# A transformer decoder on one core: written-out quantised feed-forward stages, and position rounds on two sets of PSUM banks

## What is computed

```python
att_rel_pos = jnp.einsum('bhsd,pd->bhsp', q, pos_emb_k)          # L0 attention
att_pos = jnp.take_along_axis(att_rel_pos, att_idxs[None, None, :, :].astype(jnp.int32), axis=3)
attn_val = jnp.einsum('bhsd,bhtd->bhst', q, k) + att_pos
att = jax.nn.softmax((attn_val + att_pos) * attn_scale, axis=-1)
```

```python
scale = 127.0 / jnp.clip(jnp.max(jnp.abs(x), axis=-1, keepdims=True), 1e-05)
xq = jnp.clip(jnp.round(x * scale), -128.0, 127.0) / scale
...
gate = jax.nn.silu(_bitlinear(x, w_gate))                        # L0 feed-forward
return _bitlinear(gate * _bitlinear(x, w_up), w_down)
...
h = jax.nn.gelu(bitlinear(x, w1, b1), approximate=False)         # L1 feed-forward; bitlinear
return bitlinear(h, w2, b2)                                      # normalises its input by its RMS first
```

## Time and profile before

| | us |
|---|---|
| median of three runs (1726.04 to 1728.31) | 1726.67 |
| the profiled execution | 1730.95 |
| its span, first to last instruction | 1729.2 |
| stage L0a, about | 0 to 252 |
| stage L0f, VectorE's first to last step | 385.5 to 466.9 |
| stage L1f, likewise | 879.5 to 967.3 |

### The profile page before, as it was taken

How to read it: one execution, slowest core, us unless ns; L and a number is a source line. 1 busy time by engine, 2 the same in 40 slices (tenths; PEclk the granted TensorE clock), 3 DMA queues, 4 the chain that set the end, 5 groups by cost and what they waited for, 6 DMA issues and landing times.

```text
span 1729.2 us, 24437 instructions
## 1 busy us (share of the span) xinstructions
PE 1219.0 (70%) x8742; PEld 779.5 (45%) x8754; DVE 1162.2 (67%) x2766; ACT 780.6 (45%) x1466; POOL 225.8 (13%) x170
## 2 busy tenths in 40 slices
PE   4998888974489999799933698987988920000685
PEld 2655555542357777545522354554654410000453
DVE  2655557877667887577767577686775449997354
ACT  1544355764355555346545432665342313442342
POOL 2210101300012233211111000310000000000121
PEclk7888798996789999889967676999999965555698
DMA  3000300000000000000000000000000320001100
GB/s 120 13 13 9 125 27 10 7 1 0 1 1 1 1 1 7 7 7 7 7 1 0 1 1 7 7 8 1 1 0 20 81 57 0 0 0 37 31 13 19
DMA packets 28856, 28.15 MB, mean 16 GB/s; under 512 B 12240, under 2 KB 23504, under 8 KB 27856
## 3 DMA queue, kind: packets, MB, share of 16 engines
q1 hardware_dynamic: 28752, 26.76, 5.3%
HBM read 20.20 MB, written 6.55 MB: 15 GB/s over the span
## 4 chain that ended last, share of the span: by engine, by line
PE 48%; DVE 23%; issue 14%; ACT 9%; POOL 2%; DVEq 2%; DMA 1%; SPq 1%; POOLq 0%; ACTq 0%
PE PSA L898 3%; PE PSA L888 3%; PE PSA L1323 2%; PE PSA L738 2%; DVE BIG L2622 2%; PE PSA L744 2%; PE PSA L721 2%; PE PSA L1005 2%; PE PSA L1017 2%; ACT BIG L1593 2%; PE PSA L1052 2%; DVE BIG L2614 2%; ACT QK L1600 2%; PE PSA L1061 2%; PE PSA L1296 2%
## 5 line engine op out<-in xcount | busy, mean ns | idle before, releaser
L1600 ACT ACTIVATE QK<-PSA 128x512 f32<-128x512 f32 x192 | 104.8, 595 | 110.5 <-PE PSA L898 110.3
L1353 PE MATMUL PSA<-ROWS,ONES 1*128 1x512 f32 x8 | 5.4, 760 | 205.0 <-DVE BIG L2661 205.0
L559 POOL TENSOR_TENSOR RSTD<-VEPS,HALF 128x4 f32<-128x4 f32 x41 | 41.7, 1017 | 649.0 <-DVE VEPS L1951 649.0
L2070 DVE TENSOR_TENSOR BIG<-PSA,MX 128x1024 f32<-128x1024 f32 x96 | 117.6, 1225 | 12.3 <-PE PSA L898 9.4
L888 PE MATMUL PSA<-BIG 32*128 32x512 f32 x384 | 114.6, 687 | 14.8 <-DVE BIG L2070 13.7
L2066 DVE TENSOR_REDUCE MX<-PSA 128x8 f32<-128x1024 f32 x96 | 116.8, 1217 | 6.2 <-PE PSA L888 5.6
L565 POOL TENSOR_SCALAR BIG<-BIG,COLS 128x512 f32<-128x512 f32 x52 | 80.6, 1569 | 260.7 <-ACT BIG L1585 140.3
L1593 ACT ACTIVATE BIG<-BIG 128x1024 f32<-128x1024 f32 x96 | 101.8, 1060 | 25.2 <-DVE BIG L2070 25.2
L898 PE MATMUL PSA<-K,BIG 128*128 128x128 f32 x768 | 107.1, 285 | 6.4 <-ACT BIG L1593 4.8
L898 PEld LDWEIGHTS PSA<-K,BIG 128*128 128x128 f32 x768 | 91.0, 147 | 40.5 <-ACT BIG L1593 28.5
L1353 PEld LDWEIGHTS PSA<-ROWS,ONES 1*128 1x128 f32 x8 | 1.4, 214 | 207.2 <-issue 207.1
(11 more groups left out here) (394 smaller groups left out, 3085.6 us busy)
## 6 DMA issues: line engine op xcount, KB each, us to landing
CTX<-in_ctx_t SPq DMA_DIRECT2D x16, 256.0 KB, 3.2
W<-in_w SPq DMA_DIRECT2D x1, 2048.0 KB, 7.5
W<-in_w SPq DMA_DIRECT2D x1, 1412.0 KB, 11.9
ROWS<-in_rows SPq DMA_DIRECT2D x1, 1232.0 KB, 9.2
scratch_q<-TMP SPq DMA_DIRECT2D x4, 256.0 KB, 2.0
W<-scratch_q SPq DMA_DIRECT2D x64, 16.0 KB
W<-in_w SPq DMA_DIRECT2D x2, 512.0 KB, 10.9
scratch_q<-BIG SPq DMA_DIRECT2D x4, 256.0 KB, 2.3
```

The costliest lines, as they stand in the source:

```text
L1600: act.activation(PT[:, m % 2, c, :], PS[4 + c], ACT.Copy).then_inc(p_ready.sem, 1)
L2070: dve.tensor_tensor(tile(PH[:, m % 2, :], 8), s, last(high, P), ALU.subtract).then_inc(shifted.sem, 1)
```

## The change

Position rounds: round k writes banks 0 to 3 for even k and 4 to 7 for odd k, and waits for the copies of round k-2. Round 1 waits until banks 4 to 7 are free: for a later group that is the copy of the last head product out of bank 6, which ScalarE now does ahead of its position copies. At a border TensorE's order becomes round 0, the last two products, rounds 1, 2 and 3.

Quantised stages: all passes are written out. The weights' sums move into the tail of the cross-attention ahead; the matrices are rounded one by one and TensorE waits only for those it needs. VectorE takes the next input's maximum among the hidden ones' and computes both factors at once; GpSimd computes both roots of L1f at once. TensorE transposes all four hidden tiles in a row, then two down products, the next input's transposes, the other two, and the next up products; the down products go to bank 6. On VectorE the next group's `next_normed`, and the moments of the one after it, stand ahead of the update of x. The diff, cut to what matters:

```diff
 # TensorE, L0a: positions(new, k)
+                    elif k == 1 and new:
+                        misc()
+                        pe.wait_ge(ov_ready.sem, ov_ready.at(p, 0, GB * new - 1))
...
                     else:
-                        pe.wait_ge(pos_even.sem, pos_even.at(p, new, 2 * k - 1))
-                        pe.wait_ge(pos_odd.sem, pos_odd.at(p, new, 2 * k - 1))
+                        pe.wait_ge(pos_even.sem, pos_even.at(p, new, 2 * k - 3))
+                        pe.wait_ge(pos_odd.sem, pos_odd.at(p, new, 2 * k - 3))
...
-                            mm = pe.matmul(PS[s][:, tok(half, 256)], ...
+                            mm = pe.matmul(PS[4 * (k % 2) + s][:, tok(half, 256)], ...
...
                     if more and e == HALVES - 2:
                         positions(it + 1, 0)
-                    if more and e == HALVES - 1:
-                        positions(it + 1, 2)
                     product(m)
-                    if more and e == HALVES - 2:
-                        positions(it + 1, 1)
                     if more and e == HALVES - 1:
-                        positions(it + 1, 3)
+                        for k in range(1, 4):
+                            held = positions(it + 1, k)
+                        freed = held
                         scores(m + 1)
 # ScalarE, L0a
                     if m % HALVES == HALVES - 1 and m + 1 < GROUPS * HALVES:
+                        values_out(m // 2)
                         for k in range(4):
                             positions(m // HALVES + 1, k)
-                    if m and m % 2 == 0:
+                    if m % HALVES and m % 2 == 0:
                         values_out(m // 2 - 1)
 # TensorE, L0f and L1f
+                def up(g):
+                    pe.wait_ge(xqt_ready.sem, xqt_ready.at(p, g))
+                    for i in range(GB):
+                        mm = pe.matmul(PS[i], XQT[:, tok(i)], WQ[:, 0, :], start=True, stop=True)
+                        if p == "L0f":
+                            if i == 2 and g:
+                                pe.wait_ge(x_updated.sem, x_updated.at(p, g - 1))
+                            mm = pe.matmul(PS[4 + i], XQT[:, tok(i)], WQ[:, 1, :], start=True, stop=True)
+                        mm.then_inc(h_psum.sem, 1)
...
+                input_t(0)
+                quantised_weights = sum(len(BIT_PARTS[q]) for q in quantised[:quantised.index(p) + 1])
+                pe.wait_ge(wq_ready, quantised_weights - 1)
+                up(0)
+                pe.wait_ge(wq_ready, quantised_weights)
+                for g in range(GROUPS):
+                    for i in range(GB):
+                        pe.wait_ge(hq_ready.sem, hq_ready.at(p, g, i))
+                        for c in range(4):
+                            mm = pe.transpose(PS[i][:, tok(c)], HID[:, i, tok(c)], ident)
+                        mm.then_inc(hqt_psum.sem, 1)
+                    down(g, 0)
+                    down(g, 1)
+                    if g + 1 < GROUPS:
+                        input_t(g + 1)
+                    down(g, 2)
+                    down(g, 3).then_inc(y_psum.sem, 1)
+                    if g + 1 < GROUPS:
+                        up(g + 1)
 # GpSimd, L1f
-                    root(p, 0, 0)
-                    with pool.Fori(0, GROUPS - 1) as it:
-                        ln_root(p, it)
-                        root(p, it, 1)
-                        root(p, it + 1, 0)
...
+                    ln_root(p, 0)
+                    for n in range(GROUPS + 1):
+                        pool.wait_ge(rms_stats, n + 1)
+                        pool.tensor_tensor(RR[:], VR[:], mid(HALF[:], 2), ALU.pow).then_inc(rms_root, 1)
+                        if n + 1 < GROUPS:
+                            ln_root(p, n + 1)
 # ScalarE, L1f: GELU and squares by turns, and the input's squares one group ahead
+                            act.activation(HID[:, i, :], HID[:, i, :], ACT.Gelu).then_inc(act_ready.sem, 1)
+                            if i:
+                                hidden_squares(g, i - 1)
...
+                    if p == "L1f" and g + 2 < GROUPS:
+                        input_squares(g + 2)
 # VectorE, cross_attention
+                following = run[run.index(p) + 1:][:1]
+                if following and following[0] in BIT:
+                    weight_sums(following[0])
                 normalise(GROUPS * GB - 2)
                 normalise(GROUPS * GB - 1)
 # VectorE, L0f and L1f
+                dve.drain()
+                input_magnitude()
+                if p == "L1f":
+                    dve.memset(VR[:, 1, :], 1.0)
+                    dve.wait_ge(x_squares.sem, x_squares.at(p, 0))
+                    mean_square(0, P).then_inc(rms_stats, 1)
+                next_moments(p, 0)
+                weight_scales(p)
+                quantise_weight(p, BIT_PARTS[p][0])
...
+                factors(0, 1)
+                quantise_input()
+                input_scales()
+                for m in BIT_PARTS[p][1:]:
+                    quantise_weight(p, m)
+                next_normed(p, 0)
+                next_moments(p, 1)
+
+                for g in range(GROUPS):
+                    more = g + 1 < GROUPS
...
+                        for i in range(GB):
+                            dve.wait_ge(act_ready.sem, act_ready.at(p, g, i))
+                            dve.scalar_tensor_tensor(HID[:, i, :], PS[4 + i], DQ[:, 1, i:i + 1], HID[:, i, :], ALU.mult, ALU.mult
+                                                     ).then_inc(multiplied.sem, 1)
+                            if i:
+                                magnitude(i - 1)
+                        if more:
+                            input_magnitude()
+                        magnitude(GB - 1)
...
+                    factors(0 if more else 1, 2)
+                    for i in range(GB):
+                        dve.tensor_scalar(HID[:, i, :], HID[:, i, :], QS[:, 1, i:i + 1], ROUND, ALU.mult, ALU.add).then_inc(hq_ready.sem, 1)
+                    if more:
+                        quantise_input()
+                        input_scales()
+                    dve.tensor_scalar(DQ[:, 2, :], AM[:, 1, :], WSC[:, 1, 2:3], 1.0 / 127.0, ALU.mult, ALU.mult)
+                    if more:
+                        next_normed(p, g + 1)
+                    dve.drain()
+                    if g + 2 < GROUPS:
+                        next_moments(p, g + 2)
+                    update(g)
```

More of the change, by code:

```diff
@@ L49 @@
 BIT = ("L0f", "L1f")
+BIT_PARTS = {"L0f": (0, 1, 2), "L1f": (0, 2)}
+BIT_WEIGHTS = {"L0f": ("gate", "up", "down"), "L1f": ("w1", "w1", "w2")}
 BEFORE_LOOP = -1
@@ L376, in decoder @@
         pre_ready = signal("pre_ready", {"L1f": GB})
-        squares_ready = signal("squares_ready", {"L1f": 2})
+        x_squares = signal("x_squares", {"L1f": 1})
+        h_squares = signal("h_squares", {"L1f": 1})
+        rms_stats = sem("rms_stats")
+        rms_root = sem("rms_root")
+        multiplied = signal("multiplied", {"L0f": GB})
         act_ready = signal("act_ready", {"L0f": GB, "L1f": GB, "L2f": 11, "L3t": 4})
@@ L720, in positions @@
                         for s in range(4):
-                            mm = pe.matmul(PS[s][:, tok(half, 256)], table[strip_of(s), P - 1 - 16 * m:2 * P - 1 - 16 * m],
+                            mm = pe.matmul(PS[4 * (k % 2) + s][:, tok(half, 256)], table[strip_of(s), P - 1 - 16 * m:2 * P - 1 - 16 * m],
                                            QB[strip_of(s), :, :, m], start=True, stop=True)
                     mm.then_inc(pos_psum.sem, 1)
+                    return pos_odd, pos_odd.at(p, new, 2 * k + 1)
                 def scores(m):
@@ L1149, in down @@
                     for c in range(4):
-                        mm = pe.matmul(PS[4][:, tok(i)], HQT[:, i, tok(c)], WQ[:, 2, tok(c)], start=c == 0, stop=c == 3)
+                        mm = pe.matmul(PS[6][:, tok(i)], HQT[:, i, tok(c)], WQ[:, 2, tok(c)], start=c == 0, stop=c == 3)
                     return mm
-                for i in range(GB):
-                    pe.wait_ge(hq_ready.sem, hq_ready.at(p, it, i))
-                    for c in range(4):
-                        mm = pe.transpose(PS[i][:, tok(c)], HID[:, i, tok(c)], ident)
-                    mm.then_inc(hqt_psum.sem, 1)
-                    if i:
-                        down(i - 1)
@@ L1458, in delta_tail @@
                         normed_x(it + 1)
-            bodies = {"L0f": bit_ffn, "L1f": bit_ffn,
-                      "L2f": experts}
+            bodies = {"L2f": experts}
             for p in run:
@@ L1471, in _ @@
                     pe.wait_ge(taps_ready, 1)
-                if p in ("L0f", "L1f"):
+                if p in BIT:
                     weight_means(quantised.index(p) + 1)
-                    pe.wait_ge(wq_ready, quantised.index(p) + 1)
+                    pe.wait_ge(x_updated.sem, x_updated.before[p])
+                    bit_ffn(p)
+                    continue
```

(6 more changed lines are left out.)

263 lines of the change are left out of this document (126 added, 137 removed).

## The result

The changed kernel takes 1678.42 us (median of three runs, 1676.07 to 1683.47) against 1726.67: a ratio of 0.972, 95% interval 0.970 to 0.974. Run again beside the kernel before on another chip it took 1685.47 against 1730.75, 0.9739 (0.9711 to 0.9767), 45.3 saved. The sign was right, the size was not.

The account below looks back on a forecast made before the run. A ring of dependent steps was taken to bound the quantised stages, and waits for VectorE's copies the position rounds. Savings 4.8 + 8.1 + 3.7 + 8.8 + 4.6 = 30.0 took 1726.67 to 1696.7 us; range 1685 to 1711.

Parts of the forecast that it names:

- the clock at the scores: First scores after each set of position rounds in L0a: one start of four at full clock, saving 3.7 us (0 to 14.8).
- a sum that stops at the stages whose code changes: Whole kernel: the 30.0 us saved came only from L0a and the two feed-forward stages; all other stages counted 0.
- the round's step: Position rounds in L0a: 2.1 us from round to round without a gap, saving 4.8 (first group) and 8.1 (three borders).
- first rival: L0a, first scores after each set of rounds: all four starts at full clock, 11.1 us more saved, 1685.6; chance 0.13.
- The price of a start: First scores in L0a: two slow score pairs a start, 1.85 us each, so 3.7 saved per start at full clock.
- The wait for bank 6: Borders in L0a: round 1 waits for ScalarE's copy of the last head product, 0.8 us on the path.
- L0f: First quantised feed-forward stage: 8.8 us saved, from passes 6.5, prologue 1.7 and last pass 0.6.
- L1f: Second quantised feed-forward stage: 4.6 us saved, from passes 1.0, prologue 2.5 and tail 1.1.
- The prologue's cover: Tails of L0x and L1x: idle time there covers the moved weight sums, removing 2.62 and 2.6 us from the feed-forward prologues.
- give their gain back: Rival, feed-forward passes: input transposes come 7.0 instead of 5.4 us after the first transpose, six passes lose 9.6; 1710; chance 0.18.
- the rounds overlap: Position rounds in L0a: overlap claimed; the rival without overlap loses 12.9 and 3.7 us, giving 1713; chance 0.04.
- the written-out code starves no engine: Feed-forward passes: the rival claimed new code stalls six passes, over 5.0 us each for a slower kernel, 1733 at 6; chance 0.03.

Follow-up runs that it names:

- after again: Changed kernel executed a second time, nothing edited, beside the kernel before on another chip: 1685.47 us against 1730.75, 0.9739.
- the rounds alone: Kernel before with only layer 0's position rounds on two sets of banks, feed-forward stages as before: 1706.70 us against 1731.34, 0.9851.
- the inputs first: Changed kernel with the next input's transposes ahead of the first two down products in both feed-forward stages: 1677.87 us, 0.9707 of the kernel before.
- the feed-forward filled: Changed kernel with 20 to 22 unread TensorE products a pass in both feed-forward stages: 1666.76 us against 1727.96 for the kernel before, 0.9647.
- the sums back: Changed kernel with the weights' sums back at the head of each feed-forward stage: 1686.59 us, 0.9749 of the kernel before.
- the pause filled: Changed kernel with four unread score products behind each fourth position round, ahead of the scores: 1665.60 us against 1730.75 for the kernel before, 0.9637.
- with it alone: Kernel before with only the two written-out feed-forward stages, weight sums and roots changed, position rounds as before: 1707.03 us, 0.9856.

## Why the prediction was wrong

Two steps failed: the clock at the scores, and a sum that stops at the stages whose code changes. By the stages, the first execution of the changed kernel saved 22.1 more than forecast, of which 11.3 is the clock at the scores and 6.9 lies in stages that have no term. The second saved 12.7 more, although the clock there gave 2.8 less than its term; 9.8 lies in the stages without one. The rest is the round's step and the feed-forward stages, all below.

**The clock at the scores.** The forecast took one start of four at full clock, 3.7, "since gap-free work at 46 to 50 did not raise it". L0a's saving less the 15.6 of the rounds (below) is 15.0 in the first execution of the changed kernel (0.6 of it is that round 0 starts earlier, at 22.56) and 0.9 in the second. Six executions with this L0a code (after, after again, the rounds alone, the inputs first, the feed-forward filled, the sums back: 221.88, 236.01, 232.08, 227.97, 234.19, 234.73, mean 231.1) save 21.4 on average, so the term is 5.8 on average and anything from 0.9 to 15.0 in one execution. What the argument missed: the row at 46 us shows score work that starts at half clock and stays there; it says nothing of the rounds, which come first and do raise the clock. In the kernel after:

```profile
22.56:25.60 3.04, 3.04 (x28) 2.26 (x32) 0.77 (x2) 0.77 (x2) 0.00 (x0) 0.50 0.98 256
25.60:30.30 4.70, 4.70 (x44) 1.88 (x36) 3.10 (x5) 2.49 (x5) 0.00 (x0) 1.00 1.05 418
30.30:31.80 1.50, 0.00 (x0) 0.03 (x1) 1.29 (x2) 1.09 (x2) 0.00 (x0) 1.00 1.05 287
31.80:38.00 6.20, 6.20 (x20) 3.27 (x21) 2.76 (x4) 0.28 (x1) 0.00 (x0) 0.55 0.37 68
```

In the first group the rounds, in full work, go from 0.50 to 1.00, the idle 1.50 us follows, and the clock falls into the scores. At the borders the clock is up when the rounds begin, and what differs between executions is where it falls. In the first execution it falls inside rounds 1 to 3 at all three borders, at the first at about 80.2, and is up again before the scores (first two rows). In the second, at the first border, it stays up through the rounds (last row) and falls behind them:

```profile
80.20:83.60 3.40, 2.99 (x28) 1.61 (x20) 2.27 (x5) 1.86 (x4) 0.00 (x0) 0.51 0.00 0
83.60:84.80 1.20, 0.00 (x1) 0.03 (x1) 0.94 (x2) 0.74 (x2) 0.00 (x0) 0.97 0.00 0
75.95:81.75 5.80, 5.79 (x48) 2.77 (x48) 2.58 (x4) 3.02 (x6) 0.00 (x0) 1.00 0.00 0
```

The three rounds take 5.80 and 5.79, so a fall among them costs nothing; the stretch at the scores behind them takes 4.68 in the one and 6.50 in the other. Why the fall comes that early in the first execution no run shows. With the idle time ahead of the scores worked through, the clock doesn't fall at any border. So the clock was a quantity to be bounded by both pieces, the rounds and the pause behind them. The forecast named both in its first rival and had a price for neither.

The price of a start was too small as well. The forecast counted two slow pairs of scores, but the row at 46 us is itself the third pair, in the kernel before:

```profile
45.94 2.08 PE L738 MATMUL PSA<-BIG 32*128 32x512 f32 x4
```

The third pair's products are slow at three of the four starts there (2.08, 1.52 and 2.08; 1.13 at the other). From the first scores of a group to its eighth pair the kernel before takes 30.0 to 31.6 us, and the one with the pause filled 24.6 to 26.6: 20.4 less over the four starts, where the forecast put the upper end at 14.8.

The Trainium skill, "TensorE: Matmul & The Clock Gate" (Part 1), which the prediction weighed and set aside for that row, says that sustained matmul activity releases the throttle; the extra score products agree with it (0.98 in L0a), the rounds alone agree in part, and the score work of the earlier trace rows, without a gap and at 0.50, doesn't. The same section says that how many slow products a kernel sees varies from run to run; L0a's 221.88 to 236.01 agree.

**The round's step** was 2.1 and is 1.85. The 2.03 that the forecast read at 77.66 is from a round's start to that of the head products behind it, and it is 2.03 there in the kernel after too (73.49 to 75.52). A round takes 2.10 (73.49) from first start to last end; in a row of rounds that end overlaps the next, 5.80 for three. First group 5.58 saved for 4.8 predicted; borders 3.36, 3.24 and 3.40 for 2.7. Sum 15.6 for 12.9. The wait for bank 6 (0.81 for 0.8) and its place were right.

**Stages without a term** were put at nothing without a reason, and gave 6.9 and 9.8 in the two executions. L1a and L2a gave 1.5 to 3.0 each, every time with the feed-forward change and a higher granted clock (0.95 before and 0.96 to 0.97 after in L1a, 0.73 to 0.74 and 0.78 in L2a). That the clock is the reason there is argued from the clock beside the time, not shown by an edit of its own. All behind L2x gave 1.7 and 1.8, again with the feed-forward change (1.7 with it alone, 0.6 with the rounds alone). L0x gave 0.5 and 3.0; it takes 129 to 130 us in the executions with a granted clock of 0.96 there and 132 to 133 in those with 0.94, with the sums in its tail or not (129.72 without). What sets the clock in these stages stays open.

**L0f**: 9.0 and 10.5 for 8.8. In the first execution prologue 1.85, passes 6.56, tail 0.60, for 1.7, 6.5 and 0.6. The passes are 16.15, 16.47 and 15.36 for 16.55, 16.55 and 14.95, and the waits 2.86 to 3.52 for about 3, ended by the transposes that were named. Their cause, the half clock, is shown by filling it (0.65).

**L1f**: 5.6 and 6.0 for 4.6. Prologue 2.12, passes 1.96, tail 1.51, for 2.5, 1.0, 1.1; the passes 18.85, 19.36 and 16.89 for 19.2, 19.2 and 17.6. One row the forecast didn't have: GpSimd's shared root of 128 x 8 elements takes 1.63, where one of 128 x 4 takes 1.01, so VectorE waits 1.81 for it in each pass.

**The prologue's cover** held: the sums cost nothing in the tails of the cross-attentions and 2.9 and 3.0 when put back.

**Rivals.** "All four starts at full clock", 1685.6, came true at three starts in the first execution and at none whole in the second; at all four, in the kernel with the pause filled, the starts gave 20.4 where this rival had 14.8. The feed-forward passes didn't give their gain back, the rounds overlap, and the written-out code starves no engine: in the new L0f the longest gap of VectorE marked issue is 0.28. In L1f VectorE's wait at 863.07, 2.50, bears that mark too, but TensorE's four transposes end at 862.97, so it is the same wait as in L0f; with the filling it is 0.77.

**The range** ended at 1685 because only the clock was let go beyond the forecast there. The rounds' step, L0f, L1f and the stages without a term all erred to the same side at once, by 2.7, 0.2 to 1.7, 1.0 to 1.4 and 6.9 to 9.8.

## What to carry to other kernels

Where TensorE's granted clock is low at the start of a stage, look at what it did just before, the pause included: extra products in that pause cost nothing here and brought 20 us beside the changed kernel on the same chip, and in the feed-forward passes 14 (L0f 72.42 or 70.97 to 63.48, L1f 81.94 to 75.34). Compare kernels stage by stage before believing a difference of a few us in the whole: the same code in L0a came out 14 us apart. The stages that the change doesn't edit gave 7 to 10 us here, so a sum over the edited stages alone needs a reason for the zero elsewhere. Take the step of work that runs back to back from two starts of the same work, not from a piece with other work behind it.

## What the hardware showed that was not expected

- Full work doesn't bring the clock up in every case. Score products and their transposes left no gap in the earlier trace rows and stayed at 0.50; position rounds without gaps went from 0.50 to 1.00 at 25.60, and fell from 1.00 to 0.50 at 80.20; and scores that start at full clock, with the pause ahead of them down to 0.63 at the first start, stay there (4.67 at 1.00, four times).
- With a pause of 1.5 to 1.8 us ahead of the scores, the stretch behind it took anything from 4.67 to 6.50 us; with 1.07 of that pause worked through, 4.67 each time.
- A fall of the clock costs nothing where the work hardly follows it: three rounds took 5.80 with the fall among them and 5.79 without.
- The granted clock differs between executions of one program, and with it a stage: 221.88 and 236.01.
- GpSimd's power of 128 x 8 elements takes 1.63 to 1.82, of 128 x 4 takes 1.01.
